# Dummy matmuls ahead of waits, wider expert matmuls and an earlier value projection in a four-layer kernel on one core

## The chip, the cores and the metric

The kernel runs on one core of a Trainium2 chip. The metric is the device time of one execution in microseconds (us), first instruction to last and what lies around them. TensorE has two clock levels, 1.2 and 2.4 GHz. The profile shows the granted one as a share of 2.4 GHz, so 0.50 is 1.2 GHz all the time and 1.00 is 2.4 GHz all the time.

## The reference

A block of four layers on x of 16 sequences x 256 tokens x 128 channels. In each layer x is normalised to xn and `x = x + attention(xn) + ffn(xn)`, all in f32:

```
layer 0: causal multi-query attention (16 heads of 8), then a Mamba scan (256 channels, 16 states);
         ffn: 32 experts choose 8 tokens each by softmax over tokens, merge them to one vector per
         expert and sequence, h = gelu(merged @ w1 + b1), o = h @ w2 + b2, spread back over the tokens
layer 1: causal attention, 16 heads of 64 (q, k, v projections 128 -> 1024);
         ffn: SwiGLU, width 352, inputs and weights quantised to FP4 in blocks of 16
layer 2: causal attention, 16 heads of 8; ffn: switch of 8 experts (512 wide), capacity 256, ReLU
layer 3: selective state-space scan (16 states), layer norm, linear; ffn: top 2 of 8 SwiGLU experts
         of 64, plus two shared experts
```

## The kernel before

The program is written out per engine. For each engine (TensorE `pe`, VectorE `ve`, ScalarE `ac`, GpSimd `po`, and SyncE `sp` for DMAs) there is one in-order queue, and semaphores (`k.set`, `k.at`) join them. A batch is one sequence. Layers follow one another with a drain between them. Inside a layer the work of several batches is merged in turns: each part is a generator that yields the time slot of its next step, and `merge` issues the steps of all parts in the order of these slots, ties by the order of the parts. So the slots fix the order of instructions in each queue, not their time. The slots of a turn are written out as constants: T=57 in layer 0, 48 in layer 1 (`STEP1`, `QKV1`, `V1`, `GATE1`, `HQ1`), 24 in layer 2, 37 in layer 3. PSUM has eight banks of 128x512 f32.

What the change and the prediction touch:

- Layer 0: `pe_pre0` turns the gate values (line 270) at slot 46; `pe_quad` (lines 569 to 580) makes the scores; `pe_pv` (617) multiplies by v, in two halves; `pe_results` (784) multiplies yT by w_out; `pe_sums` (761) sums the 16 states. VectorE takes maxima at line 1308.
- Between layers 0 and 1, `pe_experts0` runs 32 experts. For each, four 128x128 weight blocks of w1 (line 799) go over `merged[:, ex, :]`, 16 columns, and four blocks of w2 (line 809) over `hg`, 16 columns. An f32 matmul appears in the trace as two instructions. VectorE adds b1 (1468) and b2 (1473), ScalarE does the gelu (1906). Weights come by DMA into eight buffers (256 KB each for w1 and w2).
- Layer 1: `pe_pre1` makes q and k of the next batch in eight steps and v in four parts (line 318), all through bank 4. Each v part waits until VectorE has taken the one before (line 1006). `pe_ffn` has the gate and up projections (832, 833), the turning of the quantised h (843) and the down projection (850). VectorE quantises in `ve_fp4`, whose last instruction is line 1520. `pe_attend` issues scores (463, mask 467), turned probabilities (477), values (497) and the projection (508). In slots, the two turnings of the fifth pair stand at 34 and 34.6, its values at 38, the scores of the sixth at 40, its turnings at 42 and 42.6; the turnings of h at 42.2, 42.9 and 43.9, the last values and the down projection at 46.
- Layer 2: `pe_quad` with kind "keys" waits at its first step for a DMA that writes the maxima into the q tile (line 573 shows the wait), and `pe_max_turn` (597) waits for VectorE's last maximum.
- Layer 3: `pe_states3` sums the states in four groups a turn (line 395), each after GpSimd's product (2033). `pe_moe` has 431 to 434, 442 and 447. VectorE adds the last one's result at line 1257.
- Masks are added by bf16 matmuls of `identb` (128x128) with `mask` (128x512): lines 467, 578 and 580.

Of the kernel before, what the change touches and what calls it, by code (L numbers as in the profile page):

```python
# [204 lines left out]
STEP1, TURN1, PROJ1 = 8, 48, 8.8  # L205
QKV1, V1 = tuple(2.2 + 4.2 * j for j in range(8)), (35, 38, 41, 44.5)
GATE1, HQ1 = (14.3, 20.6), (42.2, 42.9, 43.9)
# [30 lines left out]


def pe_pre0(k, b):  # L240
    pe, w = k.pe, k.w
# [24 lines left out]
    yield 46  # L266
    bk = pe_take(k, 0)
    pe.wait_ge(*k.at("gv", b))
    for q in range(QT):
# [30 lines left out]
def pe_pre1(k, b):  # L300
    pe, w, B4, xnT = k.pe, k.w, k.bank[4], k.xnT[b % 2]
    yield 0.5
    if b:
        pe.wait_ge(*k.at("v", 1, b - 1, 3))
    pe.wait_ge(*k.at("xn", 1, b))
    for q in range(QT):
        i = pe.e.transpose(B4[:, q * P:(q + 1) * P], k.xn[b % 2][:, q, :], w["ident"])
    i.then_inc(*k.set("xn_turned", 1, b))
    for j, (n, g0) in enumerate(QK[1]):
        yield QKV1[j]  # L310
        pe.wait_ge(*(evacuated(k, 1, b, j - 1) if j else k.at("xnT", 1, b)))
        for g in range(g0, g0 + 2):
            i = pe.e.matmul(B4[:, (g - g0) * L:(g - g0 + 1) * L], w[f"w{n}1"][:, g, :], xnT[:, :], start=True, stop=True)  # L313
        i.then_inc(*k.set("qk", 1, b, j))
    for j, (q, c0, cn) in enumerate(V_PARTS[1]):
        yield V1[j]
        pe.wait_ge(*(k.at("v", 1, b, j - 1) if j else evacuated(k, 1, b, 7)))
        pe.e.matmul(B4[:, 0:cn], xnT[:, q * P:(q + 1) * P], w["wv1"][:, c0:c0 + cn], start=True, stop=True).then_inc(*k.set("v_mm", 1, b, j))  # L318
# [66 lines left out]
def pe_states3(k, b):  # L385
    pe, bk = k.pe, k.bank[SUM_BANK][:, 0:L]
    for g in range(4):
        yield STATES_AT[g] + 5.2
        if b < 0:
            continue  # L390
        pe.wait_ge(*k.at("hC", 3, b, g))
        if g == 0 and b:
            pe.wait_ge(*k.at("sT", b - 1))
        for n in range(NG):
            i = pe.e.matmul(bk, k.w["ident"], k.h[g][:, n, :], start=g == 0 and n == 0, stop=g == 3 and n == NG - 1)  # L395
        i.then_inc(*k.set("summed", 3, b, g))
# [151 lines left out]
def pe_quad(k, l, kind, b, c):  # L548
# [8 lines left out]
    if c == 0 and kind == "max":  # L557
        pe.wait_ge(*k.at("qk_act", l, b, (len(QK[l]) - 1) // 2 * 2))
        pe.wait_ge(*k.at("qk_ve", l, b, len(QK[l]) // 2 * 2 - 1))
        pe.wait_ge(*k.at("v", l, b))  # L560
    if c == 0 and kind == "keys":
        pe.wait_ge(*k.at(f"negmax{b % 2}", l, b))
    banks = [k.bank[2 * slots[r // 2] + r % 2] for r in range(4)]
    for n, g in enumerate(groups):
# [26 lines left out]
def pe_max_turn(k, l, b):  # L591
    pe = k.pe
    s = quad_slots(l, "keys", b, 0)[0]
    pe.wait_ge(*k.at(*k.slot_read[s]))
    pe.wait_ge(*k.at("mx", l, b, 2, 1))
    for q in range(QT):
# [5 lines left out]
def pe_pv(k, l, b, half):  # L602

    pe, v, bk = k.pe, k.v[b % 3], k.bank[OUT_BANK[l]]
    c = 2 * half
    pe.wait_ge(*k.at("exp", l, b, c, 1))
    pe.wait_ge(*k.at("exp", l, b, 1, 1))
    if half:
        pe.wait_ge(*k.at("oU", l, b, 0))
    elif b:  # L610
        pe.wait_ge(*(k.at("x1", l, b - 1) if l else k.at("zc", b - 1, 1)))
    for kb in range(2):
        for n in range(2):
# [162 lines left out]
def pe_results(k, b):  # L776

    pe, w = k.pe, k.w
    yield 13.1
    bk = pe_take(k, 0)  # L780
    pe.wait_ge(*k.at("yT", b))
    for q in range(QT):
# [6 lines left out]
def pe_experts0(k):  # L789
    pe = k.pe  # L790
    J = H0 // P
    for ex in range(E0 + 1):
        if ex < E0:
            s, bk = ex % 8, k.bank[ex % 2]
            pe.wait_ge(*k.at(f"w1r{s}", ex))
            if ex >= 2:
                pe.wait_ge(*k.at("hz", ex - 2))
            for j in range(J):
                i = pe.e.matmul(bk[:, j * NB:(j + 1) * NB], k.w1r[s][:, j * P:(j + 1) * P], k.merged[:, ex, :], start=True, stop=True)  # L799
            i.then_inc(*k.set("hidden0", ex))  # L800
        if ex:
            e = ex - 1
            s, bo = e % 8, k.bank[2 + e % 2]
            pe.wait_ge(*k.at("hg", e))
            pe.wait_ge(*k.at(f"w2r{s}", e))
            if e >= 2:
                pe.wait_ge(*k.at("oall", e - 2))
            for j in range(J):
                i = pe.e.matmul(bo[:, 0:NB], k.w2r[s][:, j, :], k.hg[e % 2][:, j, :], start=j == 0, stop=j == J - 1)  # L809
            i.then_inc(*k.set("output0", e))  # L810


def pe_ffn(k, b):
# [10 lines left out]
    for q in range(QT):  # L824
        yield GATE1[q]
        if q == 0:
            pe.wait_ge(*k.at("xqT", b))
            if b == 0:
                pe.wait_ge(*k.at("x_spread", 1))
        else:  # L830
            pe.wait_ge(*k.at("hh", b, q - 1))
# [627 lines left out]
def ve_experts0(k):  # L1459
    ve, w = k.ve, k.w  # L1460
    J = H0 // P
    ve.wait_ge(*k.at(*landed("wf0e")))
    for ex in range(E0 + 1):
        if ex < E0:
            ve.wait_ge(*k.at("hidden0", ex))
            if ex >= 2:
                ve.wait_ge(*k.at("hg", ex - 2))
            ve.e.tensor_tensor(k.hz[ex % 2][:, :, :], k.bank[ex % 2][:, 0:J * NB].rearrange("p (j b) -> p j b", j=J),
                               bcast(w["m_b1"][:, ex, :], NB, 2), ALU.add).then_inc(*k.set("hz", ex))
# [430 lines left out]
def ac_experts0(k):  # L1900
    ac = k.ac
    for ex in range(E0):
        ac.wait_ge(*k.at("hz", ex))
        if ex >= 2:
            ac.wait_ge(*k.at("output0", ex - 2))
        ac.e.activation(k.hg[ex % 2][:, :, :], k.hz[ex % 2][:, :, :], ACT.Gelu).then_inc(*k.set("hg", ex))

# [530 lines left out]
def build(nc, counted, ins, packed, out):  # L2438
# [24 lines left out]
    k.w2r = [k.sb("w2r", [P, H0 // P, D]) for i in range(8)]  # L2463
    k.hz, k.hg = k.two("hz", [P, H0 // P, NB]), k.two("hg", [P, H0 // P, NB])
    experts0(k, t0e, t1)
# [173 lines left out]
```

## Time and profile before

| | us |
|---|---|
| median of 3 runs (lowest, highest) | 3307.08 (3298.11, 3314.0) |
| the profiled execution | 3304.67 |
| its span, first to last instruction | 3303.4 |

The mean granted clock over the span is 0.872. Stages in the trace: loads to 24.4 us, layer 0 to 1094, its experts to 1207, the start of layer 1 to 1290, layer 1 to 2215, layer 2 to 2752 (its experts from 2695), layer 3 to 3303.4. In a row of the timeline the square bracket at the end tells how long the engine was idle before the row's first instruction and what released it. A span of n matmuls in one row includes the latency of the last one.

### The profile page before, as it was taken

The numbers are of one execution on the slowest core, as the hardware profiler recorded it, in microseconds if no ns is written. First come the engines' busy times: TensorE is split into PE (matmuls) and PEld (weight loads), VectorE is DVE, ScalarE is ACT, GpSimd is POOL, SyncE is SP. The second block draws the span as 40 slices with busy tenths as digits, with TensorE's granted clock in tenths as the row PEclk, the third lists the DMA queues.
The fourth block names the chain that finished last, engine by engine and source line by source line (L and its number), as shares of the span: only waits on it lengthen the run. The fifth ranks groups of instructions, "written<-read, shape, count | busy, mean of one in ns | idle before, by whom it ended". The sixth has DMA issues, their size and how long they took to land.

```text
span 3303.4 us, 46802 instructions
## 1 busy us (share of the span) xinstructions
PE 2491.0 (75%) x17705; PEld 1789.1 (54%) x17705; DVE 2230.6 (68%) x4585; ACT 1426.8 (43%) x3688; POOL 834.4 (25%) x453
## 2 busy tenths in 40 slices
PE   4787778787776866787878778766888876777776
PEld 2455555565554864555556555544555554454544
DVE  3588888888878133667566666644665525999887
ACT  1344444444454004555565655532333333444443
POOL 0034434334445101222222222210000001333332
PEclk9899899999998656999999999977998887888877
DMA  1001101101111530000000000000000003444342
GB/s 56 26 28 40 40 27 40 40 27 40 40 40 39 157 126 1 1 1 1 1 1 1 1 1 1 1 31 12 26 26 13 7 20 105 141 132 149 124 148 84
DMA packets 71345, 147.93 MB, mean 45 GB/s; under 512 B 6864, under 2 KB 37072, under 8 KB 70608
## 3 DMA queue, kind: packets, MB, share of 16 engines
q1 hardware_dynamic: 69072, 140.73, 12.9%
q0 software_dynamic: 2048, 4.20, 0.4%
q8 instruction: 141, 2.31, 0.3%
q14 instruction: 84, 0.69, 0.1%
HBM read 135.20 MB, written 9.18 MB: 44 GB/s over the span
## 4 chain that ended last, share of the span: by engine, by line
PE 30%; DVE 16%; issue 13%; ACT 9%; POOL 5%; DMA 2%; SPq 0%; DVEq 0%; POOLq 0%; ACTq 0%
POOL h L2033 4%; ACT pr L1743 3%; PE psum L569 2%; PE psum L497 2%; PE psum L573 2%; DVE mx L1264 2%; PE psum L508 2%; PE psum L318 2%; PE psum L463 2%; PE psum L340 2%; PE psum L809 2%; PE psum L799 2%; DVE mx L1308 1%; PE psum L761 1%; PE psum L580 1%
## 5 line engine op out<-in xcount | busy, mean ns | idle before, releaser
L1999 POOL TENSOR_TENSOR h<-h,Crep 128x1024 f32<-128x1024 f32 x128 | 383.3, 3004 | 701.8 <-DVE h L1426 701.8
L1981 POOL TENSOR_TENSOR pr<-pr,rsum 128x512 f32<-128x512 f32 x192 | 227.7, 1189 | 756.2 <-DVE rsum L1276 756.2
L1308 DVE TENSOR_REDUCE mx<-psum 128x4 f32<-128x1024 f32 (+1 forms) x192 | 229.0, 1217 | 105.8 <-PE psum L578 105.8
L1426 DVE TENSOR_TENSOR_SCAN h<-dA,h 128x1024 f32<-128x1024 f32 x128 | 290.9, 2287 | 2.4 <-ACT dA L1884 1.8
L761 PE MATMUL psum<-h,pack_wf 128*128 128x256 f32 x1024 | 259.5, 411 | 5.4 <-POOL h L1999 5.4
L2033 POOL TENSOR_TENSOR h<-h,Crep 128x1024 f32<-128x1024 f32 x64 | 150.5, 2352 | 349.3 <-DVE h L1185 349.3
L1787 ACT ACTIVATE pt<-psum 128x1024 f32<-128x1024 f32 x192 | 187.6, 1022 | 117.0 <-PE psum L580 116.9
L761 PEld LDWEIGHTS psum<-h,pack_wf 128*128 128x128 f32 x1024 | 211.3, 211 | 43.9 <-POOL h L1999 6.4
L1743 ACT ACTIVATE pr<-psum,nb 128x256 f32<-128x256 f32 (+1 forms) x512 | 211.8, 441 | 32.3 <-DVE nb L1268 32.3
L1417 DVE TENSOR_TENSOR h<-dtu,psum 128x512 f32<-128x512 f32 x256 | 164.2, 676 | 80.5 <-PE psum L748 65.6
L1884 ACT ACTIVATE dA<-delta,A 128x255 f32<-128x255 f32 x512 | 210.2, 495 | 12.1 <-DVE h L1426 10.8
L1753 ACT ACTIVATE prT<-psum 128x512 f32<-128x512 f32 x192 | 115.0, 599 | 183.9 <-PE psum L477 183.1
L395 PE MATMUL psum<-h,pack_wf 128*128 128x256 f32 x512 | 151.0, 446 | 52.7 <-POOL h L2033 51.9
L313 PE MATMUL psum<-xnT,pack_wf 128*128 128x256 f32 x512 | 153.7, 427 | 21.8 <-ACT qT L1646 15.2
L573 PE MATMUL psum<-qT,kT 32*128 32x256 f32 (+1 forms) x2048 | 129.3, 382 | 52.5 <-DMA qT<-mxT 31.0
L569 PE MATMUL psum<-kT,qT 32*128 32x128 f32 (+1 forms) x2048 | 129.7, 384 | 32.9 <-ACT pt L1787 24.4
L395 PEld LDWEIGHTS psum<-h,pack_wf 128*128 128x128 f32 x512 | 106.8, 219 | 86.1 <-POOL h L2033 71.0
L1185 DVE TENSOR_TENSOR_SCAN h<-dA,h 128x1024 f32<-128x1024 f32 x64 | 146.3, 2285 | 0.6 <-issue 0.3
L1276 DVE RECIPROCAL rsum<-sums 128x2 f32<-128x2 f32 (+1 forms) x192 | 31.9, 166 | 168.8 <-ACT pr L1743 166.5
L2008 POOL DMA_INDIRECT slots<-xn,sloti x32 | 30.8, 963 | 432.9 <-DVE sloti L1101 428.0
L1264 DVE TENSOR_REDUCE mx<-psum 128x2 f32<-128x512 f32 (+1 forms) x192 | 131.5, 685 | 6.0 <-PE psum L467 5.4
L573 PEld LDWEIGHTS psum<-qT,kT 32*128 32x128 f32 x2048 | 90.6, 207 | 78.6 <-issue 44.1
(339 smaller groups left out, 5659.1 us busy)
## 6 DMA issues: line engine op xcount, KB each, us to landing
Crep<-c_rows SPq DMA_DIRECT2D x64, 512.0 KB, 3.8
Brep<-bc_rows SPq DMA_DIRECT2D x64, 512.0 KB, 6.4
Crep<-bc_rows SPq DMA_DIRECT2D x64, 512.0 KB, 5.7
w1r<-m_w SPq DMA_DIRECT2D x32, 256.0 KB, 3.0
w2r<-m_w SPq DMA_DIRECT2D x32, 256.0 KB, 2.8
pack_wf<-wf SPq DMA_DIRECT2D x1, 3192.0 KB, 10.3
slots<-zero SPq DMA_DIRECT2D x12, 256.0 KB, 3.0
w1s<-s_w SPq DMA_DIRECT2D x8, 256.0 KB, 2.7
```

The source lines that it names most:

```text
L395: i = pe.e.matmul(bk, k.w["ident"], k.h[g][:, n, :], start=g == 0 and n == 0, stop=g == 3 and n == NG - 1)
L569: pe.e.matmul(banks[r][:, cols], qT[row:row + 32, g, q0:q0 + P], kT[row:row + 32, kg, 0:wid], start=n == 0, stop=True, skip_group_check=True)
L573: pe.e.matmul(banks[r][:, cols], kT[row:row + 32, kg, k0:k0 + P], qT[row:row + 32, g, k0:L], start=n == 0, stop=True, skip_group_check=True)
L761: i = pe.e.matmul(YB[:, c * L:(c + 1) * L], w["ident"], h[:, n, :], start=g == 0 and n == 0 and c == 0, stop=g == 3 and n == NG - 1, skip_ ...
L1264: ve.e.tensor_reduce(mx[:, 0:nh], k.bank[r][:, :].rearrange("p (h k) -> p h k", h=nh), AX.X, ALU.max).then_inc(*ve.step())
L1308: ve.e.tensor_reduce(mx[:, qb, 2 * h:2 * h + 2, groups[0]:groups[-1] + 1], k.psum[:, base:base + 2, :].rearrange("p i (n x) -> p i n x", n ...
L1426: ve.e.tensor_tensor_scan(flat(h), flat(k.dA[c][g % 2]), flat(h), 0.0, ALU.mult, ALU.add).then_inc(*k.set("scanned", 0, b, g, c))
L1743: i = ac.e.activation(pr[:, h * wid:(h + 1) * wid], bk[:, h * wid:(h + 1) * wid], ACT.Exp, bias=nb[:, h:h + 1], scale=float(HD[1]) ** -0.5 ...
L1884: i = ac.e.activation(k.dA[c][g % 2][:, n, 1:], k.delta[x % 2][:, c, 1:], ACT.Exp, scale=k.A0[:, c, g * NG + n:g * NG + n + 1])
L1981: po.e.tensor_tensor(p3, p3, bcast(k.rsum[n][:, 0:len(heads[r])], P * (q + 1), 2), ALU.mult).then_inc(*k.set("normed", 1, b, p, r))
L1999: po.e.tensor_tensor(h[:, :, :], h[:, :, :], k.Crep[n % 3][:, :, :], ALU.mult).then_inc(*k.set("hC", 0, b, g, c))
L2033: po.e.tensor_tensor(k.h[g][:, :, :], k.h[g][:, :, :], k.Crep[g][:, :, :], ALU.mult).then_inc(*k.set("hC", 3, b, g))
```

## The change

A helper `pe_idle(k, bank, n)` issues n bf16 matmuls of `identb` with the 128x512 `mask` into a bank whose content is no longer needed. Their result is never read. It is called at these places, each ahead of a wait:

- layer 0: two ahead of the wait for the gate values, four ahead of the waits of the first half of the value product (whose wait for the bank is moved in front), five ahead of the wait for yT;
- layer 1: seven ahead of the wait for xqT, and six ahead of each of the four parts of v, for all batches but the first (with a wait for `hh`, which frees bank 7);
- layer 2: seven ahead of the wait for the DMA of the maxima, six ahead of the wait for the last maximum;
- layer 3: five ahead of each group's wait for GpSimd, with the wait that bank 3 has been read.

In the experts of layer 0 each w1 matmul runs over the merged vectors of eight experts (128 columns), of which VectorE reads the 16 that belong to the expert. Each w2 matmul also runs over 128 columns; the tile `hg` gets zeroed columns behind its data for this. The four parts of v in layer 1 get earlier slots, on TensorE and on VectorE (whose slot is 1.2 later).

```diff
-QKV1, V1 = tuple(2.2 + 4.2 * j for j in range(8)), (35, 38, 41, 44.5)
+QKV1, V1 = tuple(2.2 + 4.2 * j for j in range(8)), (34.2, 36.9, 39.6, 41.8)
+def pe_idle(k, bk, n):
+    for i in range(n):
+        k.pe.e.matmul(bk[:, :], k.w["identb"], k.w["mask"], start=True, stop=True, skip_group_check=True)
...
     bk = pe_take(k, 0)
+    pe_idle(k, bk, 2)
     pe.wait_ge(*k.at("gv", b))
...
         yield V1[j]
+        if b:
+            pe.wait_ge(*k.at("hh", b - 1, 1))
+            pe_idle(k, k.bank[7], 6)
         pe.wait_ge(*(k.at("v", 1, b, j - 1) if j else evacuated(k, 1, b, 7)))
...
+        pe_idle(k, pe_take(k, 3), 5)
         pe.wait_ge(*k.at("hC", 3, b, g))
...
     if c == 0 and kind == "keys":
+        if l:
+            pe_idle(k, banks[0], 7)
         pe.wait_ge(*k.at(f"negmax{b % 2}", l, b))
...
     pe.wait_ge(*k.at(*k.slot_read[s]))
+    if l:
+        pe_idle(k, k.bank[2 * s], 6)
     pe.wait_ge(*k.at("mx", l, b, 2, 1))
...
-    pe.wait_ge(*k.at("exp", l, b, c, 1))
-    pe.wait_ge(*k.at("exp", l, b, 1, 1))
     if half:
         pe.wait_ge(*k.at("oU", l, b, 0))
     elif b:
         pe.wait_ge(*(k.at("x1", l, b - 1) if l else k.at("zc", b - 1, 1)))
+    if l == 0 and half == 0:
+        pe_idle(k, bk, 4)
+    pe.wait_ge(*k.at("exp", l, b, c, 1))
+    pe.wait_ge(*k.at("exp", l, b, 1, 1))
...
     bk = pe_take(k, 0)
+    pe_idle(k, bk, 5)
     pe.wait_ge(*k.at("yT", b))
...
-                i = pe.e.matmul(bk[:, j * NB:(j + 1) * NB], k.w1r[s][:, j * P:(j + 1) * P], k.merged[:, ex, :], start=True, stop=True)
+                i = pe.e.matmul(bk[:, j * P:(j + 1) * P], k.w1r[s][:, j * P:(j + 1) * P], flat(k.merged[:, e8:e8 + P // NB, :]),
+                                start=True, stop=True)
...
-                i = pe.e.matmul(bo[:, 0:NB], k.w2r[s][:, j, :], k.hg[e % 2][:, j, :], start=j == 0, stop=j == J - 1)
+                i = pe.e.matmul(bo[:, 0:P], k.w2r[s][:, j, :], flat(k.hg[e % 2][:, j:j + P // NB, :]), start=j == 0, stop=j == J - 1)
...
         if q == 0:
-            pe.wait_ge(*k.at("xqT", b))
             if b == 0:
                 pe.wait_ge(*k.at("x_spread", 1))
+            pe_idle(k, B6, 7)
+            pe.wait_ge(*k.at("xqT", b))
```

## Rows read from the trace of the kernel before

**Rows 1.** The page, its second part: granted clock in 40 equal slices.
```profile
PEclk9899899999998656999999999977998887888877
```
**Rows 2.** Windows, all engines, by stage; columns as in the first line.
```profile
core 0: us, PE busy (x) PEld busy (x) DVE busy (x) ACT busy (x) POOL busy (x), PEclk, DMA share, GB/s
...
24.40:1094.00 1069.60, 817.16 (x6048) 586.73 (x6048) 845.13 (x1178) 464.54 (x943) 383.27 (x128) 0.93 0.10 33
1094.00:1207.00 113.00, 109.56 (x512) 109.37 (x512) 13.24 (x65) 8.61 (x33) 0.37 (x1) 0.50 0.54 178
...
1290.00:2215.00 925.00, 719.12 (x5133) 515.18 (x5132) 586.74 (x1367) 513.05 (x1736) 225.63 (x190) 0.93 0.01 4
...
2290.00:2695.00 405.00, 328.91 (x3848) 228.48 (x3846) 227.81 (x742) 151.72 (x257) 26.79 (x28) 0.91 0.06 20
...
2752.00:3303.40 551.40, 385.46 (x1530) 263.20 (x1530) 475.80 (x968) 243.85 (x605) 186.19 (x90) 0.82 0.40 130
```
**Rows 3.** Timeline, TensorE: experts of layer 0, then a dense stretch of layer 1.
```profile
1101.98 1.87 PE L799 MATMUL psum<-merged,w1r 128*128 128x16 f32 x8
...
1105.39 1.87 PE L799 MATMUL psum<-merged,w1r 128*128 128x16 f32 x8
...
1697.68 3.74 PE L508 MATMUL psum<-pack_wf,oT 128*128 128x128 f32 x32
```
**Rows 4.** A window early in the experts of layer 0, columns as in Rows 2.
```profile
1104.00:1108.00 4.00, 4.00 (x21) 4.00 (x20) 0.52 (x3) 0.51 (x2) 0.00 (x0) 0.50 1.11 332
```
**Rows 5.** Timeline, TensorE: bf16 mask matmuls of 512 columns, low clock and high.
```profile
1280.00 1.03 PE L467 MATMUL psum<-mask,identb 128*128 128x512 bf16 x2
...
627.66 1.04 PE L578 MATMUL psum<-mask,identb 128*128 128x512 bf16 x4
...
1848.25 0.60 PE L467 MATMUL psum<-mask,identb 128*128 128x512 bf16 x2
```
**Rows 6.** Windows of two turns of layer 0, from one line 784 to the next.
```profile
598.12:658.53 60.41, 47.07 (x378) 34.49 (x379) 52.71 (x75) 28.80 (x60) 24.07 (x8) 0.97 0.11 36
658.53:721.96 63.43, 51.85 (x378) 37.52 (x378) 52.93 (x75) 28.74 (x60) 24.06 (x8) 0.89 0.11 34
```
**Rows 7.** Timeline of layer 0: two rows of TensorE and one of VectorE.
```profile
598.12 1.16 PE L784 MATMUL psum<-pack_wf,yT 128*128 128x128 f32 x8 [1.42 <-DVE yT L1452]
...
625.12 1.51 PE L617 MATMUL psum<-pt,v 128*32 128x256 f32 x32
...
628.74 1.23 DVE L1308 TENSOR_REDUCE mx<-psum 128x8 f32<-128x1024 f32 x1 [1.36 <-PE psum L578]
```
**Rows 8.** Timeline of layer 2, TensorE at the end of a turn.
```profile
2431.23 0.39 PE L597 MATMUL psum<-pack_wf,mx 128*16 128x128 f32 x2 [1.63 <-DVE mx L1308]
...
2434.02 1.15 PE L573 MATMUL psum<-qT,kT 32*128 32x256 f32 x16 [1.87 <-DMA qT<-mxT]
```
**Rows 9.** Windows of two turns of layer 2, columns as in Rows 2.
```profile
2413.50:2440.20 26.70, 22.13 (x260) 15.41 (x260) 16.22 (x55) 10.33 (x18) 1.91 (x2) 0.94 0.09 27
2440.20:2467.90 27.70, 23.12 (x260) 16.14 (x260) 16.22 (x55) 10.32 (x18) 1.91 (x2) 0.88 0.08 26
```
**Rows 10.** Waits of TensorE: who waited for whom, us in total, times, longest.
```profile
PE psum L832 <- ACT xqT L1934: 41.2, 16, 3.8
```
**Rows 11.** Timeline of layer 1 around the v parts: TensorE, last row VectorE.
```profile
1847.15 1.16 PE L463 MATMUL psum<-kT,qT 64*128 64x128 f32 x16
...
1850.31 1.13 PE L318 MATMUL psum<-pack_wf,xnT 128*128 128x512 f32 x2 [1.46 <-DVE v L1006]
...
1854.72 0.42 PE L843 MATMUL psum<-pack_wf,hq 128*96 128x128 f32 x2 [1.97 <-ACT hqT L1957]
...
1848.77 0.89 DVE L1520 SCALAR_TENSOR_TENSOR hq<-hh,f 128x704 uint32<-128x704 uint32 x1
```
**Rows 12.** Timeline of layer 3: TensorE, then VectorE.
```profile
2927.12 1.89 PE L395 MATMUL psum<-h,pack_wf 128*128 128x256 f32 x8
...
2930.17 0.29 DVE L1257 TENSOR_TENSOR X<-X,psum 128x128 f32<-128x128 f32 x1 [2.18 <-PE psum L447]
```

More of the change, by code:

```diff
@@ L560, in pe_quad @@
         pe.wait_ge(*k.at("v", l, b))
+    banks = [k.bank[2 * slots[r // 2] + r % 2] for r in range(4)]
     if c == 0 and kind == "keys":
+        if l:
+            pe_idle(k, banks[0], 7)
         pe.wait_ge(*k.at(f"negmax{b % 2}", l, b))
-    banks = [k.bank[2 * slots[r // 2] + r % 2] for r in range(4)]
     for n, g in enumerate(groups):
@@ L793, in pe_experts0 @@
         if ex < E0:
-            s, bk = ex % 8, k.bank[ex % 2]
+            s, bk, e8 = ex % 8, k.bank[ex % 2], ex // (P // NB) * (P // NB)
             pe.wait_ge(*k.at(f"w1r{s}", ex))
@@ L803, in pe_experts0 @@
             s, bo = e % 8, k.bank[2 + e % 2]
+            if e == 0:
+                pe.wait_ge(*k.at("hg_zero"))
             pe.wait_ge(*k.at("hg", e))
@@ L1461, in ve_experts0 @@
     J = H0 // P
+    for x in k.hg:
+        i = ve.e.memset(x[:, J:, :], 0.0)
+    i.then_inc(*k.set("hg_zero"))
     ve.wait_ge(*k.at(*landed("wf0e")))
@@ L1467, in ve_experts0 @@
                 ve.wait_ge(*k.at("hg", ex - 2))
-            ve.e.tensor_tensor(k.hz[ex % 2][:, :, :], k.bank[ex % 2][:, 0:J * NB].rearrange("p (j b) -> p j b", j=J),
+            ve.e.tensor_tensor(k.hz[ex % 2][:, :, :], k.bank[ex % 2].rearrange("p (j e b) -> p j e b", j=J, b=NB)[:, :, ex % (P // NB), :],
                                bcast(w["m_b1"][:, ex, :], NB, 2), ALU.add).then_inc(*k.set("hz", ex))
@@ L1905, in ac_experts0 @@
             ac.wait_ge(*k.at("output0", ex - 2))
-        ac.e.activation(k.hg[ex % 2][:, :, :], k.hz[ex % 2][:, :, :], ACT.Gelu).then_inc(*k.set("hg", ex))
+        ac.e.activation(k.hg[ex % 2][:, 0:H0 // P, :], k.hz[ex % 2][:, :, :], ACT.Gelu).then_inc(*k.set("hg", ex))
 def ac_abs(k, name, b, src, nblk):
@@ L2463, in build @@
     k.w2r = [k.sb("w2r", [P, H0 // P, D]) for i in range(8)]
-    k.hz, k.hg = k.two("hz", [P, H0 // P, NB]), k.two("hg", [P, H0 // P, NB])
+    k.hz, k.hg = k.two("hz", [P, H0 // P, NB]), k.two("hg", [P, H0 // P + P // NB - 1, NB])
     experts0(k, t0e, t1)
```

## The prediction

> **What bounds the kernel now.** I read the granted clock first, because the change adds almost nothing but TensorE work. In the page's clock row the low stretches come back all along, and one of them, two slices long, stands at 5 and 6 tenths [rows 1]. Then the windows by stage [rows 2]. The reader is to see two kinds of stage. In the experts of layer 0 TensorE is busy 109.56 of 113.00 us at a clock of 0.50, VectorE and ScalarE are nearly idle and DMA is at a share of 0.54: TensorE at 1.2 GHz is the bound. In the layers no engine is full. In layers 1 and 2 TensorE leads (719 of 925 us, 329 of 405 us), in layer 0 VectorE and TensorE are level (845 and 817 of 1070), in layer 3 VectorE leads (476 of 551). Such a stage is a loop in which the engines wait for each other in turn, so a delay counts only where somebody waits for it, and then in full. The clock there is 0.93, 0.93, 0.91 and 0.82. Before each fall TensorE was idle or had only narrow matmuls for a while; it rose again after dense work.
>
> The sum is made against the profiled execution, 3304.67 us (span 3303.4), 2.4 us under the median of 3307.08. A measurement of this kernel can tell about 0.5% (16.5 us) from no change, so faster means below 3290.6.
>
> **The price of a dummy.** Four bf16 matmuls of 512 columns take 1.04 us and two 0.60 us at the high clock, so one more costs 0.22 us. Two at the low clock take 1.03 us, so one costs about 0.4 us [rows 5]. Groups of 2, 4, 5, 6 and 7 cost 0.4, 0.9, 1.1, 1.3 and 1.5 us at the high clock.
>
> **Experts of layer 0: -49 us.** Eight instructions for w1 and eight for w2 take 3.41 us per expert (from 1101.98 to 1105.39), 0.213 us each at 0.50 [rows 3]. The same weight blocks with 128 columns run in layer 1 at 3.74 us for 32, the last one's latency of some 0.2 us taken off 0.11 us each, at the high clock [rows 3]. At the low clock that is 0.22 us, so wider matmuls cost nothing even there. I expect the clock to rise: the stretch in layer 1 with the same blocks and 128 columns is the nearest row, and it ran high. Then an expert takes 16 x 0.11 = 1.75 us. DMA is the next limit: 512 KB per expert at the 332 GB/s it reached when the buffers were empty [rows 4] is 1.58 us, just below. The loop from w1 through VectorE and ScalarE to w2 has two halves of 0.87 us as cover for about 0.8 us. The first 9 us stay as they are (loads and clock), and 29.5 of 32 experts gain 3.41 - 1.75 = 1.66 us: -49. Bounds: 2.0 us per expert if DMA lags gives -41, no start-up loss at all -53, and no rise of the clock 0. The load of layer 1's weights is issued after the last expert's, some eight experts (14 us) ahead of the end, so it stays hidden. The memset of `hg` is one short instruction ahead of a wait for a load.
>
> **Layer 0: -8 us.** The five ahead of yT (1.1 us) fit into the idle 1.42 us [rows 7]; the bank is free by then. Low clock after this place shows in turns: 60.41 us at 0.97 and 63.43 us at 0.89 [rows 6]. One turn in three is of the long kind, so without it an average turn loses 3.02 / 3 = 1.0 us: -1.0. The four ahead of the value product's first half have no idle time to hide in (the row at 625.12 has no bracket), and VectorE already waits 1.36 us for what follows it on TensorE [rows 7]: +0.9. The two ahead of the gate values fall before a wait of TensorE for ScalarE's exponentials: 0. The second low stretch of a turn (before the next batch's sums) has no dummy close ahead of it, and I take 0.4 us a turn for a better alignment. Sum -0.5 x 15 turns = -8; bounds +0.9 - 0.4 and -1.0 - 1.1 with nothing for the four: +8 to -31, of which I keep -25.
>
> **Layer 2: -21 us.** Six dummies (1.3 us) meet an idle 1.63 us, seven (1.5 us) an idle 1.87 us [rows 8]; what frees the banks is done before. Cost 0, but only while these waits last: without them it would be 2.8 us a turn. They fill the only thin place of the turn, behind which the clock falls in each turn. A turn with one low stretch takes 26.70 us, with two 27.70 [rows 9], so one stretch costs 1.0 us; an average turn, 405 us over 15 [rows 2], should come down from 27.0 to 25.7. I take 1.4 x 15 = -21, bounds -12 and -28.
>
> **Layer 1: +30 us.** The seven ahead of xqT (1.5 us) lie in a wait of 41.2 us over 16 times, 2.6 us each [rows 10]: 0, and one low stretch in five turns goes. The v parts are another matter. With the new slots the third part (39.6) comes ahead of the sixth pair's scores (40), where it came behind them (41). It waits for VectorE to take the second part, and VectorE does that only after the quantisation of h, whose last instruction ends at 1849.66 [rows 11]. So the scores, now at 1847.15, can start only after the third part at 1850.31 and its 0.9 us, 4.1 us later. Then six dummies (1.3 us) stand ahead of the fourth part, where TensorE waits for nothing. That is 5.4 us, and the stretch's own waits of 1.46 and 1.97 us [rows 11] can absorb 3.4. I take +2.0 a turn: the low stretches that the dummies take away and new ones in the new gaps are set against each other. Times 15 turns is +30. Bounds: if the order does no harm and a low stretch a turn goes (1 us), -15; if the waits absorb only 1.97 of the 5.4 us, +52.
>
> **Layer 3: +15 us.** Of four groups of five (1.1 us each), three lie in waits or ahead of one. The second stands at 2927.12, where TensorE has not waited, between the products w13 and w2; VectorE waits 2.18 us for w2's result [rows 12], and it is the fullest engine. So +1.1 a turn. The low stretch that makes this wait long comes from an idle place further ahead, which the dummies leave thin, since they stand before the sums and not behind them. If it comes 0.1 us shorter on average, +1.0 x 15 = +15. The extra wait for bank 3 is over by then; behind it are only the sums. Bounds: 0, if the low stretch goes, and +27, with half of the dummies at 0.4 us.
>
> **Sum.** -49 - 8 - 21 + 30 + 15 = -33: 3304.7 - 33 = 3272 us.
>
> One rule of the Trainium skill speaks against any of this. TensorE: Matmul & The Clock Gate, section What's actually happening, holds the ramp penalty to be under 1% of a typical kernel's span and not worth modelling. By it, at most 33 us could come back here. This trace doesn't agree for this kernel: its experts alone run 113 us at 0.50 [rows 2].
>
> **The rivals.**
> 1. The layers 1 and 3 take the dummies without harm: the scores' delay is absorbed by waits further on, as ScalarE and VectorE both idle there, and w2's wait doesn't grow. For it speaks that no engine in layer 1 is over 78% busy [rows 2]; against it that TensorE and VectorE both wait for each other inside the very stretch. Then -49 - 8 - 21 - 15 + 0 = -93: 3212 us.
> 2. On the other side: the experts' stage stays at 1.2 GHz. Place: lines 799 and 809, price 49 us. It decides from the moment that 128-column passes don't lift the clock, since they then take the same 0.213 us. Against it is the dense stretch at 1697.68 [rows 3], for it that this stage has alternated short groups and waits of its own at its start. 3272 + 49 = 3321 us, slower by 0.4%.
> 3. The change doesn't do what it says: dummies don't hold the clock up. Then layer 0 pays 0.9 x 15 = +14, layer 2 gets 0, layer 1 pays +32, layer 3 +16, and the experts, whose columns are real f32 work, still give -49: 3304.7 + 13 = 3318 us. Against it is that the mask matmuls, of the same kind, stand in dense stretches at the high clock [rows 5].
> 4. Layer 1 pays its upper bound: +52 in place of +30, 3294 us.
>
> The skill's 1% rule would lead to the third rival's side, and no figure above rests on it.
>
> **How the numbers follow.** Forecast 0.70, rival one 0.13, two 0.05, three 0.05, four 0.07. The bounds of the stages (+8/-4, +16/-17, +9/-7, +22/-45, +12/-15) add up as independent errors to about +32 and -51 around 3272. The range 3222 to 3303 takes this and rival four in, and leaves out most of rivals one, two and three, some 0.2. Faster by over 0.5%, that is below 3290.6: nine tenths of the forecast and rival one, 0.76. Slower, above 3323.6: hardly any case reaches it alone, 0.06 with the upper ends of rivals two and three. Within 0.5%: 0.18.
>
> **What the changed profile would show.** Experts: granted clock near 1.00, 1.7 to 2.0 us per expert, stage of about 65 us. Layer 0: turns of 60.9 us, VectorE's wait at 1308 grown from 1.36 to 2.2 us. Layer 2: clock near 1.00, turns of 25.7 us. Layer 1: turns of 59 us in place of 57.3, line 463 behind the third v part, VectorE waiting for it. Layer 3: VectorE's wait at 1257 up by 1.1 us. The prediction is wrong if the experts stay at 0.50, or if layer 1 gets shorter.

## The result, and the profile after

The changed kernel takes 3326.3 us where the kernel before, run beside it, takes 3305.7: a ratio of 1.0054, 95% interval 1.0036 to 1.0072. It is slower by half a per cent. The forecast was 3272, faster by 1%. The profiled execution of the changed kernel took 3327.15 us (span 3325.8), that of before 3304.67, so the two profiles differ by 22.5 us, as the medians do (20.6). One of the 13 executions of the changed kernel took 6569.3 us, is not counted and stays unexplained; the other twelve took 3307.0 to 3329.9 us.

The granted clock of the changed kernel, in 40 slices (the page's second part), against [rows 1]:

```profile
PEclk9889999999998859999999999987999997888888
```

The dip of the experts is gone. The 5 that is left lies behind them, at the start of layer 1 (a clock of 0.55 from 1164 to 1247 us); the others are single slices. The windows by stage, all engines, columns as in the first line, against [rows 2]:

```profile
core 0: us, PE busy (x) PEld busy (x) DVE busy (x) ACT busy (x) POOL busy (x), PEclk, DMA share, GB/s
24.40:1097.00 1072.60, 853.29 (x6225) 600.29 (x6225) 845.98 (x1181) 465.51 (x943) 383.44 (x128) 0.92 0.10 33
1097.00:1159.10 62.10, 61.47 (x512) 60.98 (x512) 12.94 (x63) 8.22 (x32) 0.00 (x0) 0.93 0.99 316
1105.00:1159.00 54.00, 54.00 (x481) 53.91 (x480) 12.30 (x60) 7.70 (x30) 0.00 (x0) 0.99 0.98 316
...
1240.00:2235.00 995.00, 834.80 (x5616) 576.45 (x5614) 594.12 (x1360) 517.58 (x1738) 224.97 (x190) 0.92 0.00 1
2311.00:2695.00 384.00, 350.46 (x4091) 230.18 (x4094) 232.15 (x757) 153.02 (x259) 26.87 (x28) 1.00 0.07 21
2774.00:3325.80 551.80, 436.90 (x1815) 290.48 (x1815) 455.59 (x928) 237.08 (x589) 186.51 (x90) 0.84 0.38 124
```

The stage bounds for the table below are the first w1 matmul and the last w2 matmul of layer 0's experts, the last projection of layer 1 and the end of layer 2, read from the timelines of both kernels.

| stage | before | after | difference | forecast |
|---|---|---|---|---|
| up to the experts | 1095.4 | 1097.0 | +1.6 | -8 |
| experts of layer 0 | 110.8 | 62.1 | -48.7 | -49 |
| layer 1 with its start | 999.8 | 1075.8 | +76 | +30 |
| layer 2 | 543.7 | 515.6 | -28 | -21 |
| layer 3 to the end | 553.7 | 575.3 | +21.6 | +15 |
| sum | | | +22.5 | -33 |

The experts' term held. Layer 2 gave 7 us more than foreseen, the layers 0 and 3 cost 10 and 7 us more, and layer 1 cost 46 us more. The turn lengths say the same: in layer 1 a turn took 57.49 us before and takes 62.59 after (15 turns each, from one turning of xq to the next), in layer 2 27.1 and 25.4, in layer 3 31.88 and 33.14. Single turns of the changed kernel, two of layer 0, two of layer 1, one of layer 2 and two of layer 3, columns as above:

```profile
536.97:598.40 61.43, 51.25 (x389) 36.62 (x389) 52.76 (x75) 28.91 (x60) 24.07 (x8) 0.94 0.11 36
598.40:659.84 61.44, 51.26 (x390) 36.63 (x390) 52.77 (x75) 28.92 (x60) 24.08 (x8) 0.94 0.11 36
1751.45:1813.98 62.53, 53.33 (x360) 37.13 (x358) 37.75 (x87) 33.02 (x112) 14.10 (x12) 0.92 0.00 1
1813.98:1876.84 62.86, 52.57 (x360) 35.86 (x358) 37.67 (x87) 32.80 (x112) 14.11 (x12) 0.95 0.00 1
2429.99:2455.58 25.59, 23.73 (x273) 15.66 (x273) 16.23 (x54) 10.32 (x19) 1.92 (x2) 1.00 0.09 28
2892.01:2926.73 34.72, 28.89 (x116) 19.59 (x117) 28.45 (x62) 15.38 (x40) 12.19 (x6) 0.80 0.42 128
2926.73:2960.27 33.54, 26.11 (x117) 16.92 (x117) 29.55 (x62) 15.23 (x38) 12.18 (x6) 0.90 0.43 135
```

And the stretch of layer 1 on which the forecast turned, TensorE, with ScalarE's row at its end (columns: start, duration, engine, line, operation, operands, count, idle time before and what ended it):

```profile
1844.74 1.47 PE L243 MATMUL psum<-mask,identb 128*128 128x512 bf16 x6
1848.33 1.12 PE L328 MATMUL psum<-pack_wf,xnT 128*128 128x512 f32 x2 [2.13 <-DVE v L1028]
1849.39 1.66 PE L474 MATMUL psum<-kT,qT 64*128 64x128 f32 x16
1850.98 1.04 PE L478 MATMUL psum<-mask,identb 128*128 128x512 bf16 x2
1851.81 2.20 PE L243 MATMUL psum<-mask,identb 128*128 128x512 bf16 x6
1853.84 1.02 PE L328 MATMUL psum<-pack_wf,xnT 128*128 128x512 f32 x2
1854.70 0.60 PE L488 MATMUL psum<-pack_wf,pr 128*128 128x128 f32 x4
...
1858.15 0.42 PE L865 MATMUL psum<-pack_wf,hq 128*96 128x128 f32 x2 [1.97 <-ACT hqT L1982]
```

```profile
1855.34 0.60 ACT L1778 ACTIVATE prT<-psum 128x512 f32<-128x512 f32 x1 [9.89 <-PE psum L488]
```

The third value part (L328 at 1848.33) waits 2.13 us for VectorE, the scores (L474) stand behind it, and the end of them and the dummies after them are at the low clock: the six dummies behind the scores take 2.20 us where the six ahead of the third part took 1.47. ScalarE waits 9.89 us for the turned probabilities; before it had waited 6.04 us at the same place. The last row is the one to remember: the wait of 1.97 us ahead of the third piece of hq, which the forecast let absorb a part of the delay, is 1.97 us again [rows 11].

### The profile page after: what moved, and what is told of

Read it like the earlier page. It is cut to its first block, busy times and chain, and to the rows that moved or that the text cites. A ratio compares the mean times of both kernels' runs of the same rounds, so it can differ in the third digit from the quotient of the medians.

```text
span 3325.8 us, 49102 instructions
## 1 busy us (share of the span) xinstructions
PE 2672.0 (80%) x18881; PEld 1845.4 (55%) x18881; DVE 2232.0 (67%) x4587; ACT 1431.4 (43%) x3688; POOL 834.4 (25%) x453
## 4 chain that ended last, share of the span: by engine, by line
PE 36%; DVE 21%; ACT 10%; issue 5%; DMA 1%; POOL 0%; DVEq 0%; SPq 0%; ACTq 0%; POOLq 0%
ACT pr L1768 3%; PE psum L474 2%; PE psum L243 2%; DVE mx L1286 2%; PE psum L582 2%; PE psum L519 2%; PE psum L586 2%; PE psum L350 2%; DVE h L1216 2%; PE psum L458 1%; PE psum L406 1%; PE psum L508 1%; DVE f L1536 1%; DVE mx L1330 1%; PE psum L328 1%
## 5 line engine op out<-in xcount | busy, mean ns | idle before, releaser
L243 PE MATMUL psum<-mask,identb 128*128 128x512 bf16 x1176 | 306.6, 395 | 14.9 <-DVE qT L989 7.9
L778 PE MATMUL psum<-h,pack_wf 128*128 128x256 f32 x1024 | 257.5, 408 | 5.4 <-POOL h L2024 5.4
L778 PEld LDWEIGHTS psum<-h,pack_wf 128*128 128x128 f32 x1024 | 209.1, 209 | 43.0 <-POOL h L2024 6.4
L243 PEld LDWEIGHTS psum<-mask,identb 128*128 128x128 bf16 x1176 | 111.8, 101 | 141.9 <-issue 26.7
L320 PE MATMUL psum<-xnT,pack_wf 128*128 128x256 f32 x512 | 154.8, 429 | 21.3 <-ACT qT L1671 14.6
L582 PE MATMUL psum<-kT,qT 32*128 32x128 f32 (+1 forms) x2048 | 118.4, 358 | 37.5 <-ACT pt L1812 29.0
L474 PE MATMUL psum<-kT,qT 64*128 64x256 f32 (+1 forms) x1024 | 131.1, 396 | 13.4 <-ACT pr L1768 13.4
L406 PE MATMUL psum<-h,pack_wf 128*128 128x256 f32 x512 | 130.1, 399 | 9.4 <-POOL h L2058 9.4
```

Source lines behind the costliest of these rows:

```text
L243: k.pe.e.matmul(bk[:, :], k.w["identb"], k.w["mask"], start=True, stop=True, skip_group_check=True)
L474: pe.e.matmul(k.bank[r][:, n * wid:(n + 1) * wid], qT[rows, g, q * P:(q + 1) * P], kT[rows, g, 0:wid], start=n == 0, stop=True, skip_group ...
L778: i = pe.e.matmul(YB[:, c * L:(c + 1) * L], w["ident"], h[:, n, :], start=g == 0 and n == 0 and c == 0, stop=g == 3 and n == NG - 1, skip_ ...
```

## The experiments

The experiments ran on three chips, each beside the kernel before, which took 3301.5, 3313.0 and 3317.8 us there. So ratios to it are compared across chips, and microseconds only on one. Turns are means over 15 turns of the profiled execution; TensorE's low-clock time per turn is the time at 1.2 GHz. Where dummies are taken out, the wait for the bank that they write goes with them.

### Is it the order or the dummies?

**Old places, dummies kept.** Layer 1's value parts go back to their slots, the dummies stay ahead of the first three. The fourth part has none there, since their bank is being read at that place:

```
-QKV1, V1 = ..., (34.2, 36.9, 39.6, 41.8)
+QKV1, V1 = ..., (35, 38, 41, 44.5)
...
-        if b:
+        if b and j < 3:
             pe.wait_ge(*k.at("hh", b - 1, 1))
             pe_idle(k, k.bank[7], 6)
```

> The changed kernel with the value projection's parts of layer 1 back in their places of before (the third after the scores of a turn, the fourth behind the turning of hq), the dummies kept ahead of the first three; the fourth has none, since their bank is being read there. Theory order (the third value part now stands ahead of the scores, so that these wait for VectorE's take of the second part, and the gaps left behind bring two low stretches of clock per turn): a turn of layer 1 falls from 62.55 to 57 to 58 us and the kernel takes 3240 to 3255 us. Theory dummies (the matmuls themselves, 24 per turn at 0.22 us and more, lengthen the turn wherever they stand): a turn stays at 61 to 62 us, since three quarters of them are left, and the kernel takes 3305 to 3320 us.

**New places, no dummies.** The two lines after the `if` above and the `if` itself are taken out, and the new slots stay.

> The changed kernel without the six dummies ahead of each value part of layer 1; the parts' new places stay. Theory order: the scores still wait behind the third part, a turn of layer 1 keeps at least 60 us (60 to 62.5) and the kernel takes 3290 to 3326 us. Theory dummies: a turn falls to 57 to 58 us and the kernel to 3240 to 3255 us.

**Both undone.**

> The changed kernel with the value parts of layer 1 wholly as before: old places and no dummies ahead of them; the other dummies of layer 1 (ahead of the scores, of the maxima's turn and of the first gate product) stay. Both theories that lay the stage's loss on the value parts: the turn of layer 1 falls to 56.5 to 57.5 us and the kernel to 3240 to 3250 us, as fast as the faster of the two kernels that undo one half. If instead the joined dummies of layer 1 cost the time, the turn stays above 60 us and the kernel above 3290 us.

| kernel | us | ratio to before (95%) | turn of layer 1 | low clock per turn |
|---|---|---|---|---|
| before | 3301.5 | 1 | 57.49 | 7.7 |
| changed (beside another run of before) | 3326.3 | 1.0054 (1.0036 to 1.0072) | 62.59 | 9.3 |
| old places, dummies | 3234.6 | 0.9795 (0.9767 to 0.9824) | 56.35 | 3.6 |
| new places, no dummies | 3309.3 | 1.0021 (1.0010 to 1.0032) | 61.33 | 11.2 |
| both undone | 3235.5 | 0.9803 (0.9776 to 0.9830) | 56.33 | 6.6 |

The order theory held in all three runs; in the two with old places turn and time came out a little below its ranges (56.35 and 56.33 us, 3234.6 and 3235.5). New places alone cost 61.33 - 56.33 = 5.00 us a turn; the four groups of dummies in new places cost 62.59 - 61.33 = 1.26 us more; three groups in old places cost nothing (56.35 against 56.33). No run has the fourth group in an old place or takes it away alone. The other dummies of layer 1 are worth 57.49 - 56.33 = 1.16 us a turn. So 15 x (5.00 + 1.26 - 1.16) = 76.5 us, the whole of the stage's +76. The 1.16 rests on one profile of before; with the kernel of the experts alone, whose layer 1 is that of before at 57.30 us a turn, it is 0.97.

The table has a second reading. With dummies in the old places 3.0 us a turn less are at the low clock, and the turn isn't shorter. Time at the low clock is not time lost.

### Which part's place?

**The third alone.** Against the kernel with both undone, one matmul per turn is moved:

```
-QKV1, V1 = ..., (35, 38, 41, 44.5)
+QKV1, V1 = ..., (35, 38, 39.6, 44.5)
```

> One matmul per turn of layer 1 is moved against the kernel e3_v_as_before: the value projection's third part stands ahead of the sixth pair's scores (slot 39.6 in place of 41). No dummies ahead of the parts, the other slots of before. Theory third part (this one place in TensorE's order costs the whole of the order's 5.0 us a turn, since the scores then wait for VectorE, which takes the second part only after the quantisation of h): a turn of layer 1 rises from 56.33 to 61 to 61.5 us, the kernel to 3305 to 3315 us. Rival, all slots (the earlier first, second and fourth parts, or VectorE's takes that move with them, carry a part of it): the turn stays under 60 us and the kernel under 3290.

**The other three.**

```
-QKV1, V1 = ..., (35, 38, 41, 44.5)
+QKV1, V1 = ..., (34.2, 36.9, 41, 41.8)
```

> The counterpart: first, second and fourth value part of layer 1 at the changed kernel's slots (34.2, 36.9, 41.8), the third at 41, behind the scores as before; no dummies ahead of the parts. The fourth part then stands ahead of the turning of hq. Theory third part: a turn of layer 1 stays at 56.3 to 56.8 us, the kernel at 3235 to 3243. Rival, all slots: the turn is at least 1 us longer than 56.33 and the kernel above 3250 us.

The third part alone gave 3315.0 us, a ratio of 0.9999 (0.9978 to 1.0021), and a turn of 61.38 us: as much as all the new places together. The other three gave 3276.6 us, 0.9899 (0.9851 to 0.9948), and 58.40 us a turn. That is 2.1 us more than 56.33, so here the rival's expectation held: the other places cost too when they stand alone. The two costs, 5.0 and 2.1 us, don't add up to those of all four places. Its timeline shows the place: the fourth part now stands ahead of the turned probabilities, at 1636.78, and waits 0.78 us for VectorE to take the third.

How one matmul makes 5 us shows in the two timelines. Both undone, TensorE, then ScalarE:

```profile
1622.96 2.08 PE L325 MATMUL psum<-pack_wf,xnT 128*128 128x512 f32 x2 [2.57 <-DVE v L1025]
1624.96 2.08 PE L471 MATMUL psum<-kT,qT 64*128 64x128 f32 x16
1626.98 1.04 PE L475 MATMUL psum<-mask,identb 128*128 128x512 bf16 x2
1627.81 1.83 PE L325 MATMUL psum<-pack_wf,xnT 128*128 128x512 f32 x2
1629.48 0.60 PE L485 MATMUL psum<-pack_wf,pr 128*128 128x128 f32 x4
...
1630.11 0.60 ACT L1775 ACTIVATE prT<-psum 128x512 f32<-128x512 f32 x1 [7.39 <-PE psum L485]
```

The third part ahead, TensorE, VectorE, ScalarE:

```profile
1589.23 2.08 PE L325 MATMUL psum<-pack_wf,xnT 128*128 128x512 f32 x2 [2.56 <-DVE v L1025]
1593.45 2.07 PE L325 MATMUL psum<-pack_wf,xnT 128*128 128x512 f32 x2 [2.14 <-DVE v L1025]
1595.45 2.08 PE L471 MATMUL psum<-kT,qT 64*128 64x128 f32 x16
1597.46 1.03 PE L475 MATMUL psum<-mask,identb 128*128 128x512 bf16 x2
1598.29 0.87 PE L485 MATMUL psum<-pack_wf,pr 128*128 128x128 f32 x4
...
1591.90 0.89 DVE L1542 SCALAR_TENSOR_TENSOR hq<-hh,f 128x704 uint32<-128x704 uint32 x1
1592.71 0.68 DVE L1025 TENSOR_TENSOR v<-psum,pack_wf 128x512 f32<-128x512 f32 x1
...
1598.11 0.69 DVE L1283 TENSOR_REDUCE mx<-psum 128x4 f32<-128x512 f32 x1 [1.86 <-PE psum L475]
...
1599.20 0.60 ACT L1775 ACTIVATE prT<-psum 128x512 f32<-128x512 f32 x1 [10.19 <-PE psum L485]
```

Before, the scores ran while VectorE was quantising. Now they run after it: from the second part's start to the scores it is 6.22 us in place of 2.00, 4.2 us more; the forecast had 4.1. (In the two turns shown of before and of the changed kernel the scores start 30.7 and 35.4 us after the turning of xq, 4.7 us later.) Up to the turned probabilities it is 9.06 in place of 6.52 us, since the third part no longer stands between. But VectorE waits 1.86 us for the scores and ScalarE 10.19 us in place of 7.39, and everything that follows hangs on ScalarE. Then the low clock comes on top. In this turn the fourth part and the last values stand at 0.50 and 0.58 of the clock; with both undone they stood at 1.00. Set side by side from the turning of xq on, this turn lies 2.8 us behind the longer of the two alternating turns of the kernel with both undone (56.99 us) at the turning of hq, and 4.4 us at the down product; against the shorter (55.65 us) it is 4.1 and 5.8. Either way 1.6 us of this kernel's loss come between these two places, where it is at the low clock.

The changed kernel loses the same amount by another division. Means over 15 turns, in us:

| kernel | xq to hq turned | on to the down product | on to the next xq | turn |
|---|---|---|---|---|
| before | 36.10 | 6.03 | 15.36 | 57.49 |
| both undone | 35.91 | 5.35 | 15.08 | 56.33 |
| third part ahead | 39.42 | 6.78 | 15.19 | 61.38 |
| other three moved | 37.94 | 5.06 | 15.40 | 58.40 |
| new places, no dummies | 40.74 | 4.90 | 15.69 | 61.33 |
| changed | 40.77 | 5.01 | 16.82 | 62.59 |

With all four places new, the fourth part stands ahead of hq's turning too, and nearly the whole of the order's cost, 4.8 of 5.0 us, is there before that turning. The four groups of dummies add nothing up to there and 1.13 of their 1.26 us from the down product on: TensorE is at the low clock for 3.7 us a turn behind the start of the down product, against 1.3 us without them, and the product itself takes 2.73 us on average against 1.87. A turn of the changed kernel, then one without the dummies:

```profile
1860.05 2.89 PE L872 MATMUL psum<-wdT,hqT 128*128 128x128 f32 x12 [0.46 <-ACT hqT L1982]
```

```profile
1608.84 1.60 PE L869 MATMUL psum<-wdT,hqT 128*128 128x128 f32 x12 [0.45 <-ACT hqT L1979]
```

### Layer 3 and layer 0

**Without layer 3's dummies:**

```
-        pe_idle(k, pe_take(k, 3), 5)
```

> The changed kernel without the five dummies ahead of the states' sums of layer 3. Theory of the forecast (they lie on the path at the second group and nothing else in layer 3 changed): a turn of layer 3 falls from 34.1 to about 32.4 us, the layer from 575 to about 554 us, the kernel to 3303 to 3308 us. Rival (the layer came later or its clock differs for another reason): the layer stays above 565 us and the kernel above 3315 us.

**Without those at the second group only:**

```
-        pe_idle(k, pe_take(k, 3), 5)
+        if g != 1:
+            pe_idle(k, pe_take(k, 3), 5)
```

> The changed kernel without the five dummies ahead of the states' sums of layer 3 at the second of the four groups only; the other three keep theirs. Theory of the forecast (only the second group's dummies lie on the path): the turn of layer 3 falls from 33.14 to about 31.7 us, as without any, and the kernel to 3301 to 3308 us. Rival (the dummies cost at several groups, or their moving of the low stretches costs): the turn stays above 32.3 us and the kernel above 3311 us.

Without any, 3301.4 us and a ratio of 1.0004 (0.9990 to 1.0018), a turn of 31.67 us. (The 34.1 and 32.4 us in the expectation were read from fewer turns; over all 15 it is 33.14 with all the dummies.) Without the second group's, 3313.4 us, 0.9991 (0.9964 to 1.0019), a turn of 31.75, as the forecast's theory had it; the 3301 to 3308 us expected were for the chip of the run without any, and this chip's kernel before took 3313.0. So five dummies at one of four places cost 1.4 us of the 1.47 a turn, though five of them take 1.24 us. The wait for bank 3 that goes with them was over: the changed kernel's row of the second group, at 2969.80, has no idle time before it. Two turns of the kernel without the second group's five, columns as in the windows above:

```profile
2928.97:2962.05 33.08, 25.31 (x112) 16.54 (x112) 29.52 (x62) 15.46 (x39) 12.17 (x6) 0.90 0.43 130
2962.05:2993.96 31.91, 24.76 (x111) 16.16 (x111) 29.53 (x62) 15.46 (x39) 12.18 (x6) 0.89 0.44 144
```

The clock is higher than without any dummies (means of low-clock time per turn 7.05 us against 10.70), and the turns are the same. Once more, the stretches taken away were not on the path.

**Without the four ahead of layer 0's value product:**

```
-    if l == 0 and half == 0:
-        pe_idle(k, bk, 4)
```

> The changed kernel without the four dummies ahead of the first half of layer 0's value product. Theory of the forecast (they lie on the path and cost 0.9 us in each of 15 turns, 13 us in all): the experts begin at 1084 us in place of 1097, the kernel is 13 us under the changed one, near 3313. Rival (the four also hold the clock up): the experts begin at 1092 us or later.

The experts begin at 1083.1 us. The kernel took 3321.1 us beside 3317.8 for before, 1.0010 (0.9989 to 1.0031), against 1.0054 with them: 0.44% or 14.6 us less, though the intervals nearly touch. The start of the experts is the sharper reading: in the four profiles without these dummies it is 1083.1 to 1084.0, in the eight with them 1096.3 to 1103.6, mean 1098.8. So they cost 15 us, 1.0 us a turn. The wait that carries it, of the changed kernel and then of this one:

```profile
629.89 1.23 DVE L1330 TENSOR_REDUCE mx<-psum 128x8 f32<-128x1024 f32 x1 [2.22 <-PE psum L591]
```

```profile
621.84 1.23 DVE L1328 TENSOR_REDUCE mx<-psum 128x8 f32<-128x1024 f32 x1 [1.36 <-PE psum L591]
```

### The experts alone, and the parts that pay

**Experts only.** The kernel before with the wider matmuls of `pe_experts0` and what goes with them, and no dummies.

> The kernel before with the experts' edits alone (128 columns in place of 16 for both products of layer 0's experts); no dummies anywhere. Theory of the forecast (a term of its own that carries through to the end): the stage falls from 110.8 to 60 to 62 us, the other stages keep their times within 5 us, the kernel is 49 us under the kernel before, a ratio of 0.985. Rival (the dense stretch comes at another time and the layers behind give a part back): ratio above 0.99.

3269.1 us, 0.9859 (0.9829 to 0.9888): -1.4%, or 49 us less than the kernel before on that chip. The two stages of it:

```profile
24.40:1104.80 1080.40, 827.85 (x6049) 592.78 (x6049) 845.75 (x1181) 464.44 (x943) 383.24 (x128) 0.92 0.10 33
1104.80:1167.20 62.40, 61.32 (x512) 60.83 (x512) 12.99 (x64) 8.21 (x32) 0.00 (x0) 0.93 1.00 314
```

The gain of the experts is a term of its own and goes through to the end. The first row is a caution: layer 0 is the code of before here, and the experts begin at 1104.8 us, not at 1095.4. Layer 0 alone varies by 9 us between two profiles of the same code, as much as the forecast's term for it, so the expectation that the other stages keep their times within 5 us did not hold.

**Without what costs.** The changed kernel with value parts as before, and without the dummies of layer 3's sums and of layer 0's value product.

> The changed kernel with value parts as before, and without the dummies ahead of layer 3's sums and without the four ahead of layer 0's value product; what is left are the wider matmuls of the experts and the dummies of layers 0 to 2 that lie in waits. If the costs are those read so far and add up (-91 us for the value parts, -25 for layer 3's dummies, and the forecast's -13 for the four of layer 0): 3197 to 3215 us, faster than both kernels. If layer 0's four dummies cost nothing: 3207 to 3220. If the four hold up the clock of layer 0: above 3220 us.

3201.0 us, 0.9667 (0.9622 to 0.9713). It beats both kernels by over 3%. Beside a kernel before of 3305.7 us the ratio makes 3196 us, just under the range that adds the costs up.

**Two parts.** To it, six dummies ahead of the first two value parts only, old places (`if b and j < 2:`).

> The faster version e8_joined_best with six dummies ahead of the first and the second value part of layer 1 alone, at the slots of before. Theory clock (there they lie in TensorE's waits for VectorE, 2.57 us ahead of the second part, and the sixth pair's scores, 2.08 us at 0.50 and 1.16 at 1.00, are on the path; the other dummies, ahead of the third part, were what took the gain back): a turn of layer 1 falls from 56.3 to 54.8 to 55.3 us and the kernel from a ratio of 0.967 to 0.960 to 0.963. Rival (the low stretch only moves behind the scores, as it did with dummies ahead of three parts): the turn stays at 56 us or more, the ratio at 0.966 or more.

**And in hq's wait.**

```
+        if b and j == 3:
+            yield 43.8
+            pe.wait_ge(*k.at("v", 1, b, 2))
+            pe_idle(k, B4, 6)
         yield V1[j]
```

> The same and six dummies more in the wait ahead of the third piece of hq's turning, 1.97 us long, once per turn of layer 1. Theory clock: no low stretch is left behind the scores and the turn is a further 0.5 to 1 us shorter than with the first two parts' dummies alone, since values and down product stood at 0.50 there in the kernel e1_old_slots. Rival (the wait is just used up and what follows hq's turning waits for ScalarE, not for TensorE): the same turn within 0.3 us.

The first gave 3206.9 us, 0.9661 (0.9635 to 0.9687), with a turn of 56.53: the clock theory missed, the rival held. The second gave 3195.6 us beside it, 0.9623 (0.9602 to 0.9644), with a turn of 55.82, 0.7 us less and every steady turn at 55.67: here the clock theory held. Against the kernel without what costs, which ran on another chip, the intervals of the ratios overlap, and only the turn (55.82 against 56.31 us) speaks for a gain. Two neighbouring turns of the first, and one of the second:

```profile
1577.58:1633.22 55.64, 47.74 (x347) 33.51 (x346) 36.92 (x87) 32.74 (x112) 14.15 (x12) 0.97 0.00 1
1633.22:1690.47 57.25, 48.04 (x347) 33.89 (x346) 36.91 (x87) 32.63 (x112) 14.15 (x12) 0.97 0.01 1
```

```profile
1571.79:1627.46 55.67, 49.05 (x353) 34.33 (x352) 36.92 (x87) 32.80 (x112) 14.17 (x12) 0.97 0.00 1
```

All three turns have the same mean clock of 0.97, one low stretch each, and lengths of 55.6, 57.3 and 55.7 us. What differs is where the stretch lies. In the long turn it is on the last values and the down product:

```profile
1672.66 1.98 PE L507 MATMUL psum<-prT,v 128*64 128x128 f32 x16
1674.56 2.32 PE L869 MATMUL psum<-wdT,hqT 128*128 128x128 f32 x12
```

In the short one it lies on values and a q/k step further ahead (1597.07 to 1600.53), and by the third value part nothing of it is left: both turns stand at 33.82 us there. The scores, too, at 1.16 us in place of 2.08, brought nothing, since the third part behind them still waits 1.25 us for VectorE; the kernel with both undone had no such wait. Six dummies in the wait for ScalarE keep the down product at the high clock (1.60 us), and that is worth 1.6 us in each long turn.

## Why the prediction was wrong, by its steps

**The experts, -49: right.** 62.1 us in place of 110.8, -48.7. The clock of 0.93 in the window is the start-up at 0.50. From 1105 us on TensorE is busy 54.00 of 54.00 us at a clock of 0.99, with 1.79 us per expert (forecast 1.75), so TensorE still is the bound, now at the high clock. DMA, at a share of 0.98 and 316 GB/s, is just behind it. Rival two, which had this stage stay at 1.2 GHz, is out by it, and rival three by layer 2, whose clock went to 1.00. Their 3321 and 3318 us lie nearer to the measured time than the forecast's 3272, but by chance.

**Layer 1, +30: this step failed, by 46 us.** Its order part was right in place, cause and nearly in size: the scores behind the third part, 4.1 us forecast, 4.2 measured with that part alone moved and 4.7 in the changed kernel. What failed is the next step, the absorption, and with it the clock that was put at nothing.
- The step let "the stretch's own waits of 1.46 and 1.97 us" absorb 3.4 us. The 1.46 is the wait for VectorE that moves along with the third part (2.13 us now). The 1.97 is ScalarE's work on the first two pieces of hq, which begins only when the delayed turnings are through; it is 1.97 us in every kernel that has no dummies inside it. A wait behind the delay whose releaser starts from the delayed instruction absorbs nothing. With nothing absorbed the step would have read +5.4 a turn, +81 us.
- With the third part alone moved some of the delay is made good, since that part has left its old place: of 4.2 us, 2.8 to 4.1 are left at the turning of hq. With all parts moved nothing is: there the new places stand at +4.8 us.
- That the low stretches taken away and the new ones "are set against each other" was a guess. In the changed kernel a low stretch lies on the down product and what follows, and from there to the turn's end it takes 1.5 us more than before. With the third part alone moved it lay on the fourth part and the last values, and cost 1.6 us.

Together 5.0 us a turn for the order, 1.26 for the dummies, and -1.16 for the other dummies of the layer, which the forecast had at 0. The 1.26 is near the forecast's 1.3 for the fourth group, the one in no wait, but by luck: the changed kernel comes to hq's turning no later with dummies than without (40.77 and 40.74 us), and the 1.13 us come behind the down product, with the low clock. Ahead of hq's turning, from 25 us into the turn, the dummies also took low-clock time away (2.5 us a turn in place of 6.9), so a cost of the fourth group and a gain by the clock may have cancelled there; no run separates them. The upper bound of +52, rival four, fell short too: it still let 1.97 us absorb.

**Layer 3, +15: right in place, low in size.** The second group is the place, as [rows 12] were read. It costs 1.4 us a turn where 1.1 less 0.1 stood, and 15 x 1.4 is 21 us; VectorE's wait for w2's result went from 2.18 to 3.01 us in the turn shown after. Measured from the turns it is 15 x 1.26 = 19 us against before, and the stage shows 21.6. The bound of +27 does not follow from what it names: five dummies, half of them at 0.4 us, are 1.55 us a turn, or 23 in all.

**Layer 0, -8: a small miss.** VectorE's wait went from 1.36 to 2.22 us, as forecast (2.2), and the four dummies cost 1.0 us a turn, forecast 0.9. The turns are 61.43 us throughout; the forecast had 60.9, and before the mean of three in a row was 61.4. Without the four the experts begin some 12 us earlier than in the one profile of before's code, 21 in the other. So the gaining half of the term lies between -12 and -21 where -21 stood, and the variation of this layer between profiles doesn't let it be said closer.

**Layer 2, -21: right.** The clock is 1.00 and a steady turn takes 25.59 us, forecast 25.7 (27.0 less 25.7 is 1.3, and the sum took 1.4). From one turning of the maxima to the next the mean went from 27.06 to 25.40 us, 25 us over 15 turns; on another chip, between the kernel with the experts' edits alone and the one with two parts' dummies, from 27.49 to 26.02, 22 us. What the stage's -28 has beyond the turns lies at the layer's start and end. A steady turn of layer 2 took 25.6 us in the changed kernel's profile and in the four of one chip, but 26.3 in the seven of the two other chips, at a clock of 1.00 in all. There TensorE waits up to 1.4 us for ScalarE's exponentials in place of 0.7. The dummies' lines of this layer are the same in all; why the turns differ stays open.

So the sign was lost in one term. With +76 in its place, the forecast's own sum is -33 + 46 = +13, within 10 us of what was measured.

Of the Trainium skill's rule that the ramp penalty stays under 1% of a typical kernel's span (TensorE: Matmul & The Clock Gate, What's actually happening): it stands in a passage on the ramp at the start of matmul work, and the prediction took it for all of this kernel's low clock. So taken, the runs don't agree: with the experts' edits alone 1.4% of the kernel came back with the clock. In layers 1 and 3 they bound nothing either way: 3 us a turn less at the low clock changed nothing, and 1.3 us less, taken off the last values and the down product, gave 0.7 us a turn.

## What to carry to other kernels

When an instruction is moved ahead on an in-order queue, ask what it will wait for there, and then look at each later wait that is to absorb the delay: it does only if its releaser doesn't itself start from the delayed work. Price a low clock by the place it falls on, not by its length, and put dummies only into waits that stay waits. A stage that is at the low clock and bound by TensorE, as the experts were, is the exception in which the clock is the whole price.

## What the hardware showed that was not expected

- Widening f32 matmuls from 16 to 128 columns took a stage from 110.8 to 62 us, although it makes eight times the columns: at 16 columns TensorE was busy 109.56 of 113.00 us and yet stayed at 0.50 [rows 2], at 128 it was at 0.99 from 8 us on.
- Turns with the same work and the same mean granted clock of 0.97 took 55.64 and 57.25 us, in alternation, by where the one low stretch fell.
- Removing low-clock time left the turn as it was in three places: 6.6 to 3.6 us in layer 1 (56.33 and 56.35 us), 6.8 to 3.6 us there again (56.31 and 56.53), and 10.7 to 7.05 us in layer 3 (31.67 and 31.75).
- The same turn of layer 2, at a granted clock of 1.00, took 25.6 us in five profiles and 26.3 us in seven others from other chips. Layer 0 ended anywhere between 1096.3 and 1103.6 us in eight profiles of the same code. A term of a few us can't be read from one profile each.
